# The mask of the local scores as four 64x64 quarters instead of two full products, with the unit order searched again

## What is computed

```python
bq = q.reshape(b, h, w, WINDOW, d) * QK_SCALE     # 8 heads of 64, windows of 64 queries
bk, bv = (look_around(bk), look_around(bv))        # each window sees itself and the one before: 128 keys
sim = jnp.einsum('bhwid,bhwjd->bhwij', bq, bk)
mask = (i < j) | (i > j + WINDOW) | (j == -1)
sim = jnp.where(mask, -jnp.finfo(sim.dtype).max, sim)
attn = jax.nn.softmax(sim, axis=-1)
out = jnp.einsum('bhwij,bhwjd->bhwid', attn, bv)
```

## Time and profile before

| | |
|---|---|
| median of 3 runs | 771.63 us |
| profiled execution | 777.53 us, span of its instructions 775.7 us |
| mean granted TensorE clock | 0.905 of full speed |
| TensorE matmul busy | 610.1 us (79%), 6108 products |
| VectorE / ScalarE / GpSimd busy | 560.8 (72%) / 441.6 (57%) / 236.9 us (31%) |
| chain that ended last | TensorE 44%, VectorE 24%, "issue" 13%, ScalarE 10% |

### The profile page before, as it was taken

One profiled execution on the slowest core, in us unless ns is written; L12 is line 12 of the kernel. 1 busy time (PEld: TensorE's weight loads), 2 busy tenths in 40 slices (PEclk: granted clock), 3 DMA queues, 4 the chain that ended last, 5 costly groups with the idle time before them and its releaser, 6 DMA issues.

```text
span 775.7 us, 15939 instructions
## 1 busy us (share of the span) xinstructions
PE 610.1 (79%) x6108; PEld 411.3 (53%) x6108; DVE 560.8 (72%) x1344; ACT 441.6 (57%) x1083; POOL 236.9 (31%) x153
## 2 busy tenths in 40 slices
PE   4877778979998976688797899738779986987733
PEld 3654444557656743554654657526456675564521
DVE  4858877876788556855866767688587568979886
ACT  1424306663787485457675579447855872842733
POOL 2010240433333225134253165222444323503411
PEclk9799968989999998899999999959999999795975
DMA  7380002000200200020020020002002000000001
GB/s 215 102 179 1 1 0 49 3 2 2 49 2 2 49 2 1 1 48 1 1 49 1 1 48 2 2 0 49 1 1 62 2 2 1 2 1 15 1 1 27
DMA packets 27991, 18.97 MB, mean 24 GB/s; under 512 B 14894, under 2 KB 23692, under 8 KB 27916
## 3 DMA queue, kind: packets, MB, share of 16 engines
q1 hardware_dynamic: 27196, 17.82, 9.7%
q10 hardware_dynamic: 720, 0.13, 0.1%
HBM read 9.56 MB, written 1.05 MB: 14 GB/s over the span
## 4 chain that ended last, share of the span: by engine, by line
PE 44%; DVE 24%; issue 13%; ACT 10%; SPq 4%; POOL 4%; DMA 1%; DVEq 0%; POOLq 0%; ACTq 0%
PE ps L745 7%; PE ps L816 5%; PE ps L904 4%; SPq L557 4%; PE ps L696 3%; PE ps L730 3%; PE ps L853 3%; PE ps L881 3%; ACT probs_l L1024 2%; PE ps L871 2%; PE ps L841 2%; DVE rot_b L1335 2%; PE ps L860 2%; PE ps L828 2%; ACT squares L1007 2%
## 5 line engine op out<-in xcount | busy, mean ns | idle before, releaser
L636 POOL TENSOR_TENSOR probs_l<-probs_l,row_sum_l 128x1024 f32<-128x1024 f32 x32 | 63.4, 1981 | 211.5 <-DVE row_sum_l L1363 211.4
L1024 ACT ACTIVATE probs_l<-ps,neg_max_l 128x128 f32<-128x128 f32 x256 | 90.8, 379 | 12.4 <-DVE neg_max_l L1355 12.2
L816 PE MATMUL ps<-wqkv,hT_l 128*128 128x512 f32 x128 | 72.1, 646 | 23.6 <-DVE rot_b L1335 21.3
L629 POOL TENSOR_TENSOR rot_a<-rot_a,rot_b 128x1024 f32<-128x1024 f32 x32 | 76.7, 2400 | 39.3 <-DVE rot_b L1335 39.3
L1334 DVE TENSOR_TENSOR rot_a<-ps,rot 128x512 f32<-128x512 f32 x64 | 44.1, 689 | 52.0 <-ACT squares L1007 50.6
L1007 ACT ACTIVATE squares<-ps 128x512 f32<-128x512 f32 x64 | 38.4, 600 | 63.5 <-PE ps L816 52.7
L696 PE MATMUL ps<-k_diag,hT 32*128 32x308 f32 x256 | 62.7, 535 | 14.3 <-DVE probs L1202 6.5
L968 ACT ACTIVATE probsT<-ps 128x512 f32<-128x512 f32 (+1 forms) x96 | 47.3, 529 | 35.3 <-PE ps L730 35.2
L904 PE MATMUL ps<-hT_f,w 128*128 128x512 f32 x96 | 54.4, 650 | 9.8 <-ACT gelu_g L1057 5.3
L957 ACT ACTIVATE probs<-probs 128x1232 f32<-128x1232 f32 x32 | 39.4, 1232 | 32.7 <-DVE probs L1202 18.8
L730 PE MATMUL ps<-ident,probs 128*128 128x128 f32 x320 | 51.5, 296 | 6.6 <-ACT probs L957 1.9
(11 more groups left out here) (165 smaller groups left out, 1382.1 us busy)
## 6 DMA issues: line engine op xcount, KB each, us to landing
v_win<-v_win SPq DMA_DIRECT2D x56, 128.0 KB, 2.3
score_bias<-fside_1x16xSxS SPq DMA_DIRECT2D x4, 616.0 KB, 8.3
wqkv<-L_ffn_wqkv SPq DMA_DIRECT2D x2, 768.0 KB
x_res<-x SPq DMA_DIRECT2D x4, 256.0 KB
w<-L_ffn_w SPq DMA_DIRECT2D x6, 128.0 KB
out<-x_res SPq DMA_DIRECT2D x3, 256.0 KB, 2.4
rot_a<-L_ffn_w SPq DMA_DIRECT2D x2, 256.0 KB, 4.1
probs_l<-c_rot SPq DMA_DIRECT2D x1, 512.0 KB
```

What stands on the lines that cost most here:

```text
L629: g.tensor_tensor(rot_a[:, t], rot_a[:, t], rot_b[:, t % 2], ALU.add).then_inc(rot_added.sem, 1)
L636: g.tensor_tensor(w, w, row_sum_l[:, t].unsqueeze(2).to_broadcast([P, LH, P]), ALU.mult).then_inc(probs_ready.sem, 1)
L816: mm(to, hl[:, tile(t)], wqkv[:, l, k * INNER:(k + 1) * INNER], start=True, stop=True).then_inc(ps.fill(it, "QK", t, k), 1)
L1024: last = a(probs_l[:, t % 2, tile(hd)], ps.bank(it, "S", t, half)[:, tile(c)], ACT.Exp, bias=neg_max_l[:, t, hd:hd + 1], accum_out=row_sum ...
```

## The change

The two full mask products of a score unit are replaced by four on 64x64 tiles of the array, each with 64 rows of the identity and of the mask, 64 queries as output and 512 columns. Quarter (half, j) uses the rows `half` of the array, writes the window `j` of bank `half`, and so stands on the same array tile as the score products that add to it. The mask table's first variant becomes the same for both halves of the rows, and a quarter picks its variant by the number of its window (0 for the sequence's first window alone). All five order strings are replaced; each engine has the same units as before.

```diff
 ORDER = {
     "sync":
-        "U2 Z2 U12 Z2 U18 Z2 W1 Z2",
+        "Z4 U32 Z3 W1 Z1",
...
     "vector":
...
                     to = [opens(it, "S", t, half) for half in halves]
-                    masked = mask[:, min(t, 1)].unsqueeze(1).to_broadcast([P, CH, P])
-                    for half in halves:
-                        mm(to[half].rearrange("p (c k) -> p c k", c=CH), ident_b, masked, start=True, stop=False, skip_group_check=True)
+                    for j in halves:
+                        for half, heads in enumerate((lo, hi)):
+                            masked = mask[heads, min(2 * t + j, 1)].unsqueeze(1).to_broadcast([WIN, CH, P])
+                            mm(to[half][j * WIN:(j + 1) * WIN].rearrange("p (c k) -> p c k", c=CH), ident_b[heads, heads], masked,
+                               start=True, stop=False, tile_position=(WIN * half, WIN * j), skip_group_check=True)
                     for c in range(CH):
...
-    before_first = (np.arange(P)[:, None] < WIN) & (k < WIN)
+    before_first = k < WIN
```

## The result

The changed kernel took 761.78 us, the median of 4 runs (759.77 to 765.62), the kernel before 771.69 beside it (771.13 to 775.67): ratio 0.9853, 95% interval 0.9812 to 0.9895. Run once more among the experiments it was 759.85 us, with the kernel before at 774.63 there: ratio 0.9808 (0.9791 to 0.9825). The median of the kernel before lies between 771.6 and 775.8 us over all comparisons, so ratios are compared from here on, each against the kernel before on the same chip. The forecast was 766.5 us, 0.66% faster; measured were 1.5 to 1.9%.

What follows compares the result with a forecast made beforehand. TensorE was taken to bind most of the local-score stretch. Saving 0.25 us on 32 tiles gives 8.0 us; times 0.64, 5.1; the order adds zero: 771.6 - 5.1 = 766.5 us, range 760.5 to 774.5.

Steps and rivals of the forecast that it cites:

- What bounds the kernel, and the mask's price: Local-score stretch of 519 us: TensorE binds most of the time, 84% busy; a tile pays 0.60 us up to its first score.
- The step to tiles: TensorE going from the full array to 64x64 tiles: 0.10 us, moved ahead of the mask and not removed.
- How much reaches the end: Share of TensorE's saved 8.0 us that shortens the run: 0.64, the middle of 44% and 84%, giving 5.1 us.
- The re-searched order I put at zero: All engines' new strings: no gain or loss, as most units stayed or moved by one and no count changed.
- the order gains too: Rival, chance 0.13: new strings use a twentieth of TensorE's 82 us idle time, 4 us more, 762.
- the row maximum T46: VectorE example of order gain: it stood at 495.98 us though its scores were done since 489.4; now four units earlier.
- The rival of late handovers: Rival, chance 0.12: small units moved back delay GpSimd's multiplies and TensorE's transposes; four exposed cost 7.6 us, 774.2.
- U27: Reciprocals on VectorE, moved behind the sum ending at 494.4: GpSimd's multiply left 0.3 us of slack where there were 15.
- T74: Four exponentials on ScalarE, moved behind copies ending at 537.8: they end at 539.3, no slack before the reciprocals.
- Quarters one by one: Rival, chance 0.05: the mask's quarters run singly on TensorE, 0.96 us against 0.60 per tile, 7.4 us slower, 779.
- two by two: Case within a rival of chance 0.13 (gain does not arrive): quarters run in pairs, 0.53 against 0.60, 1.4 us gained, 771.
- Head and tail keep their lengths, 46 table loads: Signs of being right: stretches before and after the local scores unchanged in length, ScalarE's table loads again 46.

Runs made afterwards that it cites:

- the swapped order: Changed kernel with quarters issued (0,0), (0,64), (64,0), (64,64), the second in the first's row group: 760.23 us, ratio 0.982 to the kernel before.

## Why the prediction was wrong

- **What bounds the kernel, and the mask's price: right.** Start distances gave 0.60 us up to the first score, and 0.24 + 0.10 to which it falls; the list's busy time (19.1 to 13.1 us) would have told 6 us of it. The step to tiles moved ahead of the mask at 0.10, as summed. Missed were the few ns between quarters and 0.05 us behind the scores; with these a tile saves 0.31 us where 0.25 was summed, 9.9 us in all instead of 8.0.
- **"How much reaches the end", 0.64: not refuted for the old strings, but without a mechanism.** Quarters alone gave 4 us (0.52%, interval 2.4 to 5.6) against 5.1 summed. The middle between two bounds landed near by luck: one share does not hold. It is 0.6 for added work, 0.4 to 0.5 for the step that was made, about 0 beyond it, and the sum had no term for the clock, which was 0.902 without a mask and 0.916 with a doubled one.
- **"The re-searched order I put at zero": the step that failed.** It measured 7 us alone and 11 with quarters (0.9948 to 0.9808). My reasons were that most units kept their place or moved by one and that no count changed. Both were true, and neither bears on waits or on the granted clock: 282 of TensorE's 606 units had moved, in a stretch with 82 us of idle time and 51 us at the lower clock. Between the quarters alone and the changed kernel the idle time fell by 5 us and the busy time of the same products by 5. Which moved units do it stays open. The rival "the order gains too" named this and priced it at 4 us with a chance of 0.13, after one example. That example was right in its place: the row maximum T46 now runs at 475.53, 0.48 us after VectorE began to wait for it, instead of 6.6 us after its scores were done.
- **The rival of late handovers: wrong in its places.** I had compared the new place on one engine with the old times of the others. U27 did move behind the sum (482.98), GpSimd's multiply ended at 485.2, but TensorE's L861 that needs it came at 495.98: its turn had moved as well, and there are 11 us of slack. T74 ran at 522.44 to 523.86, and the squares behind it waited 0.26 us for TensorE, exactly as before.
- **Quarters one by one, or two by two: wrong**, shown by the trace and by the swapped order. (The first one's sum was also off by a little: 4 x 0.21 + 0.10 is 0.94, not 0.96.) In the Trainium skill, "TensorE: Matmul & The Clock Gate", Packing small matmuls, starts some 4 ns apart are stated, and the 0.41 us seen here agrees; its sentence on row groups does not.
- **Head and tail keep their lengths, 46 table loads: right.**

## What to carry to other kernels

Price a reordered schedule from the idle time of the engine that leads and its time at the lower clock, not from how far its units moved, and never at zero with a narrow range: here it was worth more than the edit it came with. A shorter operation inside a fixed order paid only part of what it saved (4 of 8 to 10 us) and paid 8 under the order searched again; the two belong together, and each should be run alone to see which one paid. When a stretch gets shorter or fails to, compare the busy time of the products that did not change: if it moved, so did the clock. Before a stretch of one profile is explained, see how much it differs between profiles of the same strings. When a unit moves on one engine, look where the units that give to it and take from it moved on the others before calling it late.

## What was not expected of the hardware

Four bf16 products of 64x64 tiles and 512 columns take 0.41 us together where each lasts 0.40, in either order of the tiles, and the scores that add to them start 0.24 us after the first. The weight loads of 64 columns for all four fit in as well: in the changed kernel the first load for the scores starts 0.03 us after the first quarter.

```profile
196.46 0.11 PEld L836 LDWEIGHTS ps<-mask,ident_b 64*64 64x64 bf16 x4 [0.17 <-issue]
196.49 1.01 PEld L842 LDWEIGHTS ps<-kT_l,qT_l 64*64 64x64 f32 x32
```

And with the mask taken out the granted clock fell: under the old strings its mean over all executions was 0.916 with the mask doubled, 0.906 to 0.909 with full products, 0.908 with quarters and 0.902 with none, so part of what shorter work saves was paid back in a slower clock.
